# A Taylor-gated layer on one Trainium2 core: delta kept in its PSUM bank, x's buffer released earlier, maxima in other banks

## The reference

```python
approx_up = x @ up_w.T                       # "u", 128 wide
delta = x @ gate_w.T - local_point           # 128 wide
keep = (abs(delta) <= 2.5)
approx_out = approx_up @ local_approx_output.T
for m in 1..6:
    dterm = exp(log|delta| * m - discount[m-1]) * (sign if m is odd)   # delta**m * factor
    tmp = dterm * approx_up;  if m > 4: tmp *= keep
    approx_out += tmp @ fuse_weight[:, :, m-1].T
ffn = (silu(x @ Wg.T) * (x @ Wu.T)) @ Wd.T   # hidden width 1248
x1 = layernorm(x + approx_out + ffn)
```

## Time and profile before

| | |
|---|---|
| Runs | 799.52 us median of 3 (799.33 to 799.72) |
| The profiled execution | 801.41 us, of which its span is 799.6 |
| Mean granted clock of PE | 0.984 |
| PE busy | 760.3 us (95%), 3814 matmuls |
| DVE busy | 503.9 us (63%) |
| ACT busy | 224.9 us (28%) |
| POOL busy | 179.0 us (22%) |

### The profile page before, as it was taken

One profiled execution on the slowest core, in us unless ns is written; L12 is line 12 of the kernel. 1 busy time (PEld: TensorE's weight loads), 2 busy tenths in 40 slices (PEclk: granted clock), 3 DMA queues, 4 the chain that ended last, 5 costly groups with the idle time before them and its releaser, 6 DMA issues.

```text
span 799.6 us, 12815 instructions
## 1 busy us (share of the span) xinstructions
PE 760.3 (95%) x3814; PEld 358.7 (45%) x3814; DVE 503.9 (63%) x861; ACT 224.9 (28%) x352; POOL 179.0 (22%) x144
## 2 busy tenths in 40 slices
PE   6979998899999999999999999999999999999994
PEld 2434343344434444444444444454445444444441
DVE  4997997668786678677777788535654461125105
ACT  1533355443832221222222222122212212122220
POOL 0525744511111111111111121221212221222210
PEclk9989999999999999999999999999999999999997
DMA  8539000431000000000000000000100010001001
GB/s 314 223 110 349 0 1 0 164 153 52 1 1 1 0 0 1 0 0 0 0 1 1 0 0 1 2 1 1 52 0 0 0 53 0 0 1 53 0 0 52
DMA packets 9247, 31.83 MB, mean 40 GB/s; under 512 B 896, under 2 KB 1536, under 8 KB 8320
## 3 DMA queue, kind: packets, MB, share of 16 engines
q1 hardware_dynamic: 9216, 31.42, 10.4%
HBM read 27.22 MB, written 4.19 MB: 39 GB/s over the span
## 4 chain that ended last, share of the span: by engine, by line
PE 78%; DVE 11%; issue 5%; ACT 2%; DMA 2%; SPq 1%; DVEq 0%; ACTq 0%
PE acc L376 28%; PE pa L364 20%; PE pb L364 19%; PE acc L429 4%; DMA big<-in_x_t 2%; DVE work L1043 1%; PE pick_b L463 1%; DVE big L1220 1%; PE pick_a L453 1%; DVE small L1146 1%; DVE big L945 1%; PE pa L569 1%; PE pick_a L471 1%; PE pb L569 1%; PE pick_b L471 1%
## 5 line engine op out<-in xcount | busy, mean ns | idle before, releaser
L376 PE MATMUL acc<-big,work 128*128 128x512 f16 (+1 forms) x1128 | 254.9, 379 | 0.1
L854 POOL TENSOR_TENSOR work<-work 128x512 f32 (+1 forms) x96 | 116.0, 1209 | 531.9 <-ACT work L760 286.6
L364 PE MATMUL pa<-xs,big 128*128 128x512 f16 (+1 forms) x816 | 188.9, 381 | 7.2 <-DVE big L945 3.0
L364 PE MATMUL pb<-xs,big 128*128 128x512 f16 (+1 forms) x816 | 188.7, 381 | 4.0 <-DVE work L1129 4.0
L376 PEld LDWEIGHTS acc<-big,work 128*128 (+1 forms) x1128 | 108.8, 98 | 124.1 <-issue 1.5
L364 PEld LDWEIGHTS pa<-xs,big 128*128 128x128 f16 (+1 forms) x816 | 79.1, 98 | 102.8 <-issue 11.6
L364 PEld LDWEIGHTS pb<-xs,big 128*128 128x128 f16 (+1 forms) x816 | 79.2, 98 | 95.4 <-issue 7.4
L1317 DVE TENSOR_TENSOR big<-rev,winner 128x1024 bf16<-128x1024 f16 x28 | 34.1, 1219 | 76.6 <-PE pb L569 76.6
L429 PE MATMUL acc<-big 128*128 128x512 f16 x336 | 73.6, 379 | 1.7 <-ACT big L680 1.1
L827 ACT ACTIVATE work<-pa 128x512 f32<-128x512 f32 x28 | 16.7, 597 | 180.2 <-PE pa L569 180.2
L760 ACT ACTIVATE work<-work 128x512 f32 (+1 forms) x40 | 25.2, 630 | 115.0 <-DVE work L1129 115.0
(11 more groups left out here) (124 smaller groups left out, 654.3 us busy)
## 6 DMA issues: line engine op xcount, KB each, us to landing
big<-in_w_all SPq DMA_DIRECT2D x2, 3840.0 KB, 19.5
rows<-in_x SPq DMA_DIRECT2D x4, 1024.0 KB, 10.9
big<-in_w_all SPq DMA_DIRECT2D x2, 1536.0 KB, 8.0
out<-rows SPq DMA_DIRECT2D x3, 1024.0 KB, 4.3
big<-in_x_t SPq DMA_DIRECT2D x8, 256.0 KB, 6.4
big<-in_x_t SPq DMA_DIRECT2D x2, 1024.0 KB, 7.5
big<-in_w_all SPq DMA_DIRECT2D x1, 2048.0 KB, 14.4
big<-in_w_all SPq DMA_DIRECT2D x2, 1024.0 KB, 9.5
```

What stands on the lines that cost most here:

```text
L364: mm = nc.tensor.matmul(dst[:, :], weights(wp)(kc * P, P), x_part16(g, xp, kc), start=(kc == 0 and wp == xp), stop=(stop and kc == KC - 1 ...
L376: mm = nc.tensor.matmul(acc[t][:, :], act_part(pair, j, ap, t * P, P), weights(wp)(0, H), start=(first and ap == wp), stop=(last and ap == 1))
L854: nc.gpsimd.tensor_tensor(act_part(pair, j, 1), act32[j], act_part(pair, j, 0), ALU.subtract).then_inc(act_lo, 1)
```

## The change

In words:

- delta stays in PSUM. ACT writes its absolute value to SBUF (`delta_size`), and delta with its bias back into the bank it was read from. The products of terms 1 to 4 read that bank.
- The masked delta for terms 5 and 6 is made by one DVE operation (`keep_delta`, in place of two), written into u's bank, and made just ahead of term 5 and no longer ahead of the scales.
- x_hi(0) moves on ACT between terms 4 and 5 of group 0; x_low(0) on DVE stands directly behind group 0's terms. x_max(1), the small constants and c1's maximum, which stood there, go behind group 1's bounds; the maximum of w1's first part goes between group 1's terms 4 and 5.
- Since the banks hold delta, PE puts the maxima elsewhere: group 0's into acc3, t_part(1) alone into pb ahead of group 0's last term, x_part(1) and c1's into pa behind it, groups 2 and 3's ahead of terms 6 and 5 of the group before into the bank of a delta that is used up. PE waits there for all terms of the group made (`terms_ready`), and the next products wait until the scale is read (`t_scaled`).
- Group 2 makes delta ahead of u. x comes in four loads for each group.
- The final copy in `bound_terms` goes.

```diff
-PEAK_PARTS = (2, 5, 7, 9, 10, 11)
-PEAK_W1, PEAK_W2 = GROUPS, GROUPS + 1
+PEAK_PARTS = (2, 3, 5, 7, 9, 10, 11)
+PEAK_X1, PEAK_W1, PEAK_W2 = 2, GROUPS + 1, GROUPS + 2
...
-        delta, keep, delta_keep = [work32[:, (RING + i) * GT:(RING + i + 1) * GT] for i in range(3)]
+        delta_size = work32[:, RING * GT:(RING + 1) * GT]
...
             def load_xt(g):
-                sp.dma_start(xt[g % 2].rearrange("p (k t) -> p k t", k=KC),
-                             x_t[:, :, g * GT:(g + 1) * GT]).then_inc(xt_in[g % 2], 16)
+                for kc in range(KC):
+                    sp.dma_start(xt[g % 2][:, kc * GT:(kc + 1) * GT], x_t[:, kc, g * GT:(g + 1) * GT]).then_inc(xt_in[g][kc], 16)
...
-            def group_peaks(g):
-
-                pe.wait_ge(delta_ready, g + 1)
-                parts = [x_part[:, g:g + 1], t_part[:, g:g + 1]]
-                if g == 1:
-                    parts.append(c1_part)
-                peaks(g, parts, delta_bank(g))
+            def group_peaks(g, m):
+
+                if g == 0 and m == 5:
+                    pe.wait_ge(terms_ready, G)
+                    peaks(1, [t_part[:, 1:2]], delta_bank(0))
+                elif g == 0 and m == G:
+                    peaks(PEAK_X1, [x_part[:, 1:2], c1_part], u_bank(0))
+                elif g and m == (0, 5, 4, 5)[g]:
+                    pe.wait_ge(terms_ready, (g + 1) * G)
+                    if g + 1 < GROUPS:
+                        peaks(g + 2, [x_part[:, g + 1:g + 2], t_part[:, g + 1:g + 2]], delta_bank(g))
+                    else:
+                        peaks(PEAK_W1, [w_part[:, 0:1]], pb)
...
                 if g >= 2:
-                    pe.wait_ge(xt_in[g % 2], 16)
-                    pe.wait_ge(u_copied, g - 1)
-                    pe.wait_ge(delta_ready, g - 1)
-                for dst, col, done in ((u_bank(g), 0, u_ready), (delta_bank(g), S, delta_pre_ready)):
+                    pe.wait_ge(terms_ready, (g - 1) * G)
+                products = ((u_bank(g), 0, u_ready), (delta_bank(g), S, delta_pre_ready))
+                for i, (dst, col, done) in enumerate(products if g != 2 else products[::-1]):
+                    if g >= 2:
+                        pe.wait_ge(t_scaled, g)
+                    if g == 2 and i:
+                        pe.wait_ge(x_scaled, 2)
+                    if g == 2 and i:
+                        pe.wait_ge(c1_scaled, 1)
...
                     if col == 0 and g == 1:
-                        group_peaks(0)
+                        pe.wait_ge(delta_ready, 1)
+                        peaks(0, [x_part[:, 0:1], t_part[:, 0:1]], acc[TPG - 1])
...
-                    if g + 1 < GROUPS and m == (4 if g == 2 else G):
-                        group_peaks(g + 1)
-                    if g == 3 and m == 5:
-                        peaks(PEAK_W1, [w_part[:, 0:1]], pick_b)
+                    group_peaks(g, m)
...
-                act.activation(delta, delta_bank(g)[:, :], ACT.Identity, bias=point_sb[:, 0:1]).then_inc(delta_ready, 1)
+                act.activation(delta_size, delta_bank(g)[:, :], ACT.Abs, bias=point_sb[:, 0:1]).then_inc(delta_sized, 1)
+                act.activation(delta_bank(g)[:, :], delta_bank(g)[:, :], ACT.Identity, bias=point_sb[:, 0:1]).then_inc(delta_ready, 1)
...
+                    if g == 0 and m == 4:
+                        x_hi(0, 0)
...
             make_delta(1)
-            x_hi(0, 0)
             copy_sums(0)
...
-                v.tensor_copy(t_part[:, g:g + 1], d_two).then_inc(max_part, 1)
-                step(v.scalar_tensor_tensor(out=keep, in0=delta, scalar=-THD, in1=delta, op0=ALU.is_ge, op1=ALU.mult))
-                settle()
-                step(v.scalar_tensor_tensor(out=delta_keep, in0=delta, scalar=THD, in1=keep, op0=ALU.is_le, op1=ALU.mult))
+
+            def bound_sums(g):
+
+                settle()
+                v.scalar_tensor_tensor(out=t_part[:, g:g + 1], in0=d_two, scalar=f_inv, in1=u_max, op0=ALU.mult,
+                                       op1=ALU.mult).then_inc(max_part, 1)
+
+            def keep_delta(g):
+
+                dve.wait_ge(delta_sized, g + 1)
+                step(v.scalar_tensor_tensor(out=u_bank(g)[:, :], in0=delta_size, scalar=THD, in1=delta_bank(g)[:, :],
+                                            op0=ALU.is_le, op1=ALU.mult))
...
                     if m == 5:
+                        keep_delta(g)
                         settle()
-                    v.tensor_tensor(term[n % RING], term[(n - 1) % RING], delta_keep if m >= 5 else delta,
+                    v.tensor_tensor(term[n % RING], term[(n - 1) % RING], (u_bank if m >= 5 else delta_bank)(g)[:, :],
                                     ALU.mult).then_inc(terms_ready, 1)
...
             for g in range(GROUPS):
-                if g == 1:
-                    x_low(0)
                 if g >= 2:
                     x_max(g)
                 measure(g)
+                bound_terms(g)
                 if g == 0:
                     fuse_max(2)
                     scale_fuse()
-                bound_terms(g)
-                if g in (1, 2):
-                    w1_max(g - 1)
-                scale_terms(g)
-                power_scales(peak[:, 0:1], x_exp[:, g:g + 1], x_scale[:, g:g + 1], x_inv[:, g:g + 1], x_scaled)
-                if g == 0:
-                    fuse_low(0)
-                make_terms(g)
-                if g == 0:
+                bound_sums(g)
+                if g == 1:
                     x_max(1)
                     small_constants()
                     dve.wait_ge(small_in, 16)
                     v.tensor_reduce(c1_part, c1_raw, axis=AX.X, op=ALU.max, apply_absolute_value=True).then_inc(max_part, 1)
+                if g == 2:
+                    w1_max(1)
+                scale_terms(g)
+                if g == 1:
+                    peaks(PEAK_X1, 2, u_bank(0))
+                power_scales(peak[:, 0:1], x_exp[:, g:g + 1], x_scale[:, g:g + 1], x_inv[:, g:g + 1], x_scaled)
+                if g == 0:
+                    fuse_low(0)
+                if g == 1:
+                    scale_c1()
+                make_terms(g)
+                if g == 0:
+                    x_low(0)
```

More of the change, by code:

```diff
@@ L235, in program @@
         vectors_in, const_in, small_in, c2_in = [sem(n) for n in ("vectors_in", "const_in", "small_in", "c2_in")]
-        first_in = [sem(f"first_in{kc}") for kc in range(KC)]
-        second_in = [sem(f"second_in{kc}") for kc in range(KC)]
-        xt_in = [sem("xt_in0"), sem("xt_in1")]
+        ug_in = [sem(f"ug_in{kc}") for kc in range(KC)]
+        xt_in = [[sem(f"xt_in{g}_{kc}") for kc in range(KC)] for g in range(GROUPS)]
         rows_in = [sem(f"rows_in{g}") for g in range(GROUPS)]
@@ L318, in _ @@
             sp.dma_start(const_sb[:, :], consts).then_inc(const_in, 16)
-            for kc in range(KC):
-                sp.dma_start(xt[1][:, kc * GT:(kc + 1) * GT], x_t[:, kc, GT:2 * GT]).then_inc(second_in[kc], 16)
+            load_xt(1)
             sp.dma_start(c1_raw, c1_rep).then_inc(small_in, 16)
@@ L949, in scale_phase1 @@
             def scale_phase1():
-                peaks(PEAK_W1, 1, pick_b)
+                peaks(PEAK_W1, 1, pb)
                 power_scales(peak[:, 0:1], w_exp[:, 0:1], w_scale[:, 0:1], w_inv[:, 0:1], w_scaled)
@@ L987, in x_max @@
             def x_max(g):
-                if g < 2:
-                    for kc in range(KC):
-                        dve.wait_ge(*((first_in[kc], 32), (second_in[kc], 16))[g])
-                else:
-                    dve.wait_ge(xt_in[g % 2], 16)
+                for kc in range(KC):
+                    dve.wait_ge(xt_in[g][kc], 16)
                 v.tensor_reduce(x_part[:, g:g + 1], xt[g % 2], axis=AX.X, op=ALU.max,
@@ L1002, in measure @@
                     fuse_max(1)
-                dve.wait_ge(delta_ready, g + 1)
-                step(v.tensor_reduce(d_max, delta, axis=AX.X, op=ALU.max, apply_absolute_value=True))
+                dve.wait_ge(delta_sized, g + 1)
+                step(v.tensor_reduce(d_max, delta_size, axis=AX.X, op=ALU.max))
             def bound_terms(g):
@@ L1036, in make_terms @@
                         dve.wait_ge(u_copied, g + 1)
+                        dve.wait_ge(delta_ready, g + 1)
                     else:
@@ L1060, in between_terms @@
                         x_low(1)
-                    elif m == 3:
-                        scale_c1()
+                    elif m == 4:
+                        w1_max(0)
                     elif m == 6:
@@ L1082, in scale_c1 @@
             def scale_c1():
-                power_scales(peak[:, 2:3], c1_exp, c1_scale, c1_inv, c1_scaled)
+                power_scales(peak[:, 1:2], c1_exp, c1_scale, c1_inv, c1_scaled)
             def low_c1():
@@ L1090, in low_c1 @@
                                        in1=c1_parts[:, 0:KC * P], op0=ALU.mult, op1=ALU.subtract).then_inc(c1_lo, 1)
+            dve.wait_ge(vectors_in, 16 * 2)
```

(10 more changed lines are left out.)

23 lines of the change are left out of this document (12 added, 11 removed).

## The result

The changed kernel takes 788.66 us, the median of four runs (788.14 to 791.37), where the kernel before has 799.62 beside it (799.33 to 799.82). The ratio is 0.9869, with a 95% interval of 0.9849 to 0.9888. The forecast was 791.6, a ratio of 0.990, in a range of 789.3 to 797.0. (The ratios here are the measured ones over the single runs and not those of the medians: by the medians a0's would be 0.9884.) Its eight runs in all fall into two groups: five of 788.0 to 789.1 and three of 791.4 to 791.8, whose mean granted clock is 0.988 where the others have 0.992 to 0.994. What makes the difference is told under a0.

What follows compares the result with a forecast made beforehand. Before 128.4 us PE waits on VectorE's chain plus one transfer; behind it PE is busy. Gains 6.3, less 1.6, plus 1.9, plus 1.3 make 7.9 us: 799.52 to 791.6, range 789.3 to 797.0.

Steps and rivals of the forecast that it cites:

- The price of a term: VectorE's products with delta in PSUM: 0.75 us each, also beside GpSimd, where two SBUF inputs had stretched to 1.64.
- Rival 4: VectorE's products on PSUM cost more even with GpSimd idle; gain gone at 1.13 us each, 804 at 1.64; chance 0.04.
- Group 0: Earlier end of VectorE's chain and earlier x load (39.7): group 1's terms at 53.15 instead of 59.41, ahead by 6.3.
- rival 1: A PSUM operand doesn't free VectorE's products from GpSimd: gain only 2.1 to 2.8 us, 797.0; chance 0.13.
- Rival 3: PE still waits for x's transfer at group 2's products: 792.7, or about 792.5 with floors paid in turn; chance 0.09.
- The new wait of 1.5: After group 1's last term (71.8), PE waits 1.5 us for t_scaled, since w1_max(1) stands ahead of the scale.
- 1 to 2 us that I had named as a sign: Sign of a right forecast: PE waits that long for VectorE's scale near 72.
- rival 2: VectorE has slack counted as used, so the 1.5 us wait and small ones go: gain 9.5 to 10.5, 789.5; chance 0.10.
- Groups 2 and 3: Shorter PE waits: 1.9 us gained at group 3's maxima (99.91), 1.3 more on the way to its terms (106.84).
- From the maxima to PE's next start 6.0 us as before: The stretch from w1's maxima to the first SwiGLU matmul (122.42 to 128.43) keeps its length.
- Behind it all waits are relative: After the first SwiGLU matmul, forecast 7.9 us earlier at 120.5, all waits, DMAs included, simply move along.
- Rival 5: One clock fall more or less, like those at 50.66 or 128.43, moves any case by 1.8 us; no chance given.

Runs made afterwards that it cites:

- a0: The changed kernel, unedited, run again in a later set of four: median 790.37 us, ratio 0.9872.
- e1: The changed kernel with delta and the masked delta in SBUF again, orders, loads and places of the maxima kept: 796.69 us, ratio 0.9957.
- e2: The changed kernel with x_max(1), the constants and c1's maximum ahead of x_low(0) again, group 1's maxima waiting for all three parts: 791.51 us, ratio 0.9904.
- e3: The changed kernel with x of groups 2 and 3 in one load of 1 MB each: 789.72 us, ratio 0.9873.
- e5: The changed kernel with w1_max(1) behind the scales of group 2 instead of ahead of them: 787.51 us, ratio 0.9844.
- e10: The changed kernel with GpSimd's four row additions of group 2 between its last four terms of group 3, not behind them: 785.3 us, ratio 0.982.
- e9: The kernel before with x_hi(0) between group 0's terms 4 and 5 and x_low(0) ahead of x_max(1), delta in SBUF: 799.78 us, ratio 0.9994.
- e6: The changed kernel with w1's first low part ahead of the four small products for the sums: 787.28 us, ratio 0.9843.
- e7: The kernel before with w1's first low part ahead of the four small products for the sums: 800.11 us, ratio 1.0002.

## What the prediction had right, and the step that failed

In order of its steps, each with what it forecast and what was measured from T0 on.

- **The price of a term.** 0.75 was forecast, 0.68 measured, also beside POOL, and `keep_delta` at 0.684. e1 shows by taking it away that this is the change's main effect: 5.6 of the 9.0 us up to w1's maxima, 8.0 of the 11.0 in all by the medians (with the hand-off and the clock behind it). Without it the new order still gains: e1's ratio is 0.9957. Rival 4, a PSUM product that is dearer by itself, is refuted by the same rows. Two slips in the working change nothing: two of the four operations of L1004 ran beside POOL, not one, and all are as flat; and rival 4's 21 operations at 1.64 would add up to 810, not 804.
- **Group 0.** The load was forecast for 13.3 behind T0 (39.7 less 26.43) and went out at 13.4 (38.21 less 24.80). Group 1's terms were forecast 26.7 behind T0 (53.15) and started 26.4 behind it (51.21). The gain is 6.57 instead of 6.3, and the clock fall behind the old hole is gone, as forecast: 1.00 in that stretch. Of it 1.96 is the products' (in e1 group 1's terms start 28.37 behind T0), where rival 1 had 1.9. The new place of x_max(1) and c1's maximum gives 1.8 (e2), through t_part(1). Rival 3, the load, did not come to pass with four pieces and did, for a wait of 1.59, with one (e3).
- **The new wait of 1.5.** It exists, at the place named, and e5 shows that w1_max(1) is its cause. It was 0.77, below the 1 to 2 us that I had named as a sign: from T0, PE's terms ended 0.2 earlier than forecast (45.15 and 45.37), and the products behind DVE's scale started 1.0 earlier (45.92 and 46.92). A faster line of terms was the reason that I had given for rival 2.
- **Groups 2 and 3.** 1.9 up to the maxima of 99.91 and 1.3 on the way to 106.84 were forecast, 2.11 and 1.31 measured.
- **The step that failed** is this term of the sum: "From the maxima to PE's next start 6.0 us as before", with "Behind it all waits are relative". I had carried the part from 122.42 to 146 over as a block. The hand-off measured 5.23 and not 6.0, and the way behind it was 1.30 shorter and not the same. Together that is 2.1 of the 3.2 us that the sum lacks: 0.78 because POOL's rows now start earlier relative to the maxima and hold up one operation of DVE less (shown by e10, which removes the overlap and gains 1.65 there), and 1.30 because in this profile the clock did not fall behind the hole, which is 2.26 instead of 3.03. That second half is luck and can't be counted on in every run: in a0's profile it fell behind the same hole, and the median of that set, 790.37, lies inside the range. Rival 5 had the mechanism and its size (1.8 stated, 1.34 measured at the join), but no chance of its own, and so no share in the range, which ended at 789.3 (rival 2's own 10.5 would have put that end at 789.0). The other 1.1 are the new wait and the products around it (0.6: forecast to cost 1.6 up to group 2's terms, measured 1.0), group 0 (0.3) and group 3's maxima (0.2).

What stays open is what decides whether the clock falls behind a hole of 2.3 to 2.8 us or near 16 us, and how long it stays low (5.47 and 6.57 for one product behind holes of 4.06 and 4.04). Each is worth 1.1 to 1.7 us in these profiles, and the runs of the kernel after lie up to 3.8 apart (788.00 to 791.76).

## What to carry to other kernels

When a VectorE product on two SBUF tensors shows a wide spread at one shape, look for GpSimd beside it, and ask whether one operand already lies in PSUM and can stay there: here this alone was worth about 1% of the kernel. A freed buffer pays only if the engine that is late next gets faster too (e9 gained 0.4 on PE's way and nothing that the times show), and an earlier start pays only if the engines that feed it move with it (e6 and e7 against e10). And a part "behind the change" should be read for its overlaps as well: the same GpSimd work falling 1.2 us earlier took one stretched step and, with luck, a clock fall out of it. Where single runs differ by 3 us, compare the lengths between fixed points of the timeline, not the medians alone (e6 and e10).

## What the runs showed of the hardware

- A VectorE product of one PSUM and one SBUF input costs no more than two SBUF inputs: 0.669 to 0.690 us for 128x512 float32, where the undisturbed minimum with both in SBUF was 0.677. One that also writes to PSUM (`keep_delta`): 0.678 to 0.687.
- Beside the same GpSimd instructions, VectorE's TENSOR_SCALAR on 1 column (int32) keeps its 0.15 us, and on 4 columns (float32) it takes 0.85 to 1.31 instead of 0.22 to 0.23. Whether the size or the type makes the difference, no run separates. The Trainium skill, SBUF — State Buffer, "Who interferes with whom", says that `tensor_scalar` can enter a two-port mode, in which it contends with GpSimd, and that whoever issues second is blocked for the whole of the other's instruction; the operations on 4 columns agree (0.90 and 1.31, ending with GpSimd's), though no trace shows their mode, and those on 1 column weren't held.
- The granted clock fell in or behind the idle stretch of PE ahead of the SwiGLU part in two of six profiles where that was 2.26 to 2.80 us, and in four of four where it was 3.03 to 3.47. Behind the join's stretch of 2.65 us it fell in 13 of 14. A fall ahead of the SwiGLU part lengthened the first twelve matmuls by 1.7 us (4.44 instead of 2.75), and 1.34 of it was left at the join (a0 against after).
